# A Griffin block and an MLP in fp32 halves: eight even rounds per chunk, the second FFN ten rounds behind the first

## What is computed

```python
def _L0_attn_ref(x, norm1_w, Wx, Wy, conv_w, conv_b, Wi, Wa, lam, Wo, norm2_w, Wg, Wu, Wd):
    t = rmsnorm(x, norm1_w)
    xb = causal_depthwise_conv(t @ Wx, conv_w, conv_b)      # 4 taps
    r = sigmoid(xb @ Wa); i = sigmoid(xb @ Wi)
    a = exp(-8 * softplus(lam) * r)
    b = sqrt(maximum(1 - a * a, 1e-12)) * (i * xb)
    h = scan of h[s] = a[s] * h[s-1] + b[s] over the tokens
    h1 = x + (h * gelu(t @ Wy)) @ Wo
    u = rmsnorm(h1, norm2_w)
    return h1 + (gelu(u @ Wg) * (u @ Wu)) @ Wd              # 256 -> 1024 -> 256

x = layernorm(x + _L0_attn_ref(x, ...))
x = layernorm(x + relu(x @ W1 + b1) @ W2 + b2)              # 256 -> 1024 -> 256
```

## Time and profile before

| | |
|---|---|
| median of 3 runs | 683.96 us (678.43 to 684.47) |
| the profiled execution | 684.14 us, span 682.3 us, granted clock 0.974 |
| busy: TensorE, VectorE, GpSimd, ScalarE | 625.8, 425.5, 284.6, 252.9 us |
| first gate product of chunk 0 | 60.8 us |
| on the chain that ended last | PE 59%, DVE 22%, ACT 9%, issue 6%, POOL 2% |

### The profile page before, as it was taken

How to read it: one execution, slowest core, us unless ns; L and a number is a source line. 1 busy time by engine, 2 the same in 40 slices (tenths; PEclk the granted TensorE clock), 3 DMA queues, 4 the chain that set the end, 5 groups by cost and what they waited for, 6 DMA issues and landing times.

```text
span 682.3 us, 10001 instructions
## 1 busy us (share of the span) xinstructions
PE 625.8 (92%) x3689; PEld 553.2 (81%) x3689; DVE 425.5 (62%) x704; ACT 252.9 (37%) x484; POOL 284.6 (42%) x399
## 2 busy tenths in 40 slices
PE   7878999899989999899988999899998999898786
PEld 7777897888878898788978898788988888786766
DVE  5993568556695567656595466755595566854332
ACT  5523237223550328223461337323372336411030
POOL 2934415541364514543263423734165413643141
PEclk9989999899999999899998999899998999999989
DMA  8400000000100001000000000000000000000000
GB/s 293 162 1 2 0 32 1 1 31 2 32 1 30 3 1 32 1 31 1 32 0 18 16 1 32 0 32 1 32 0 1 32 1 0 1 33 0 1 1 31
DMA packets 13067, 15.71 MB, mean 23 GB/s; under 512 B 584, under 2 KB 12256, under 8 KB 13024
## 3 DMA queue, kind: packets, MB, share of 16 engines
q1 hardware_dynamic: 13024, 15.09, 6.5%
HBM read 10.89 MB, written 4.19 MB: 22 GB/s over the span
## 4 chain that ended last, share of the span: by engine, by line
PE 59%; DVE 22%; ACT 9%; issue 6%; POOL 2%; POOLq 0%; DVEq 0%; ACTq 0%
PE psum L303 12%; PE psum L305 11%; PE psum L304 11%; PE psum L314 8%; PE psum L316 8%; PE psum L315 8%; DVE units_lo L748 7%; DVE xv L680 2%; DVE uT_lo L695 2%; ACT decay L514 2%; DVE gy L689 2%; DVE row L720 2%; DVE uT_lo L632 1%; PE psum L324 1%; ACT L533 1%
## 5 line engine op out<-in xcount | busy, mean ns | idle before, releaser
L946 POOL TENSOR_SCALAR units_hi<-ring 128x512 fp32r<-128x512 f32 x128 | 115.4, 911 | 140.3 <-DVE ring L743 101.7
L748 DVE TENSOR_TENSOR units_lo<-ring,units_hi 128x512 fp32r<-128x512 f32 x128 | 104.6, 839 | 16.2 <-POOL units_hi L946 16.2
L314 PE MATMUL psum<-w_hi,units_hi 128*128 128x256 f32 x256 | 77.4, 302 | 20.1 <-DVE units_lo L748 20.1
L743 DVE TENSOR_TENSOR ring<-psum,ring 128x512 f32<-128x512 f32 x64 | 44.2, 691 | 79.8 <-PE psum L305 79.8
L554 ACT ACTIVATE ring<-psum 128x512 f32<-128x512 f32 x64 | 38.2, 597 | 133.0 <-PE psum L305 94.8
L316 PE MATMUL psum<-w_hi,units_lo 128*128 128x256 f32 x256 | 76.1, 297 | 0.0
L315 PE MATMUL psum<-w_lo,units_hi 128*128 128x256 f32 x256 | 76.0, 297 | 0.0
L314 PE MATMUL psum<-w_d_hi,units_hi 128*128 128x256 f32 x256 | 72.5, 283 | 2.7 <-DVE units_lo L748 2.7
L316 PE MATMUL psum<-w_d_hi,units_lo 128*128 128x256 f32 x256 | 71.6, 280 | 0.0
L315 PE MATMUL psum<-w_d_lo,units_hi 128*128 128x256 f32 x256 | 71.6, 280 | 0.0
L314 PEld LDWEIGHTS psum<-w_hi,units_hi 128*128 128x128 f32 x256 | 52.8, 206 | 22.0 <-DVE units_lo L748 22.0
(11 more groups left out here) (140 smaller groups left out, 1549.0 us busy)
## 6 DMA issues: line engine op xcount, KB each, us to landing
xs<-in_L_attn_x_dram SPq DMA_DIRECT2D x8, 512.0 KB, 3.5
out_dram<-row SPq DMA_DIRECT2D x16, 256.0 KB, 2.1
raw_weights<-in_L_ffn_W_dram SPq DMA_DIRECT2D x2, 1024.0 KB, 7.2
raw_weights<-in_L_attn_Wg_dram SPq DMA_DIRECT2D x1, 1024.0 KB, 7.9
raw_weights<-in_L_attn_Wu_dram SPq DMA_DIRECT2D x1, 1024.0 KB, 10.0
raw_weights<-in_L_attn_Wd_dram SPq DMA_DIRECT2D x1, 1024.0 KB, 12.7
raw_weights<-in_L_attn_Wx_dram SPq DMA_DIRECT2D x1, 256.0 KB, 2.7
raw_weights<-in_L_attn_Wy_dram SPq DMA_DIRECT2D x1, 256.0 KB, 3.0
```

The lines of the kernel that those rows point to most:

```text
L314: nc.tensor.matmul(dst, hi[:, k, toks], w_hi[n][:, k, :], start=(k == 0), stop=False)
L743: nc.vector.tensor_tensor(ring[:, m % RING, :], psum[2 * (m % 2) + 1][:, :], ring[:, m % RING, :], ALU.mult).then_inc(gu_ready, 1)
L748: nc.vector.tensor_tensor(units_lo[:, m, :], ring[:, m % RING, :], units_hi[:, m, :].bitcast(FP32), ALU.subtract).then_inc(ready, 1)
L946: nc.gpsimd.tensor_scalar(units_hi[:, m, :], ring[:, m % RING, :], 1.0, 0.0, ALU.mult, ALU.add).then_inc(ready, 1)
```

## The change

The loops and `period` are gone. Every engine walks through rounds r = 8p + m, written out without a loop: p is the period and m the unit. In round r TensorE makes the gate and up products of unit r, takes unit r-1 down (`down`), makes the W1 product of unit r-10 (`mlp_up`, `LAG_UP`) and takes unit r-11 down through W2 (`mlp_down`, `LAG_DOWN`). Wd and W2 accumulate unit by unit, each in two banks of its own. The mixing of chunk p+1 is laid out over the rounds of period p: transposes of t and Wx in round 0, Wa and Wi in 3, Wy in 4, Wo in 5, transposes of u in 7 (in period 0, Wo and the transposes of u both in 7). Transposes of x1 of chunk p-1 stand in round 1. Eleven rounds follow the last unit of the first FFN.

The gate now has bank 0 alone, and up and W1 share bank 1, until the last rounds, in which W1 alternates between 0 and 1. The ring of four and the eight units are replaced by two slots for each FFN: `gu_raw`, `gu_hi`, `gu_lo` and `hid_raw`, `hid_hi`, `hid_lo`. x1 has halves of its own, and `h1`, `row` and the layernorm's small tiles are doubled; h1 + x is kept in `h1`. GpSimd copies the high halves of both FFNs (`gate_hi`, `hidden_hi`), and VectorE subtracts (`gate_lo`, `hidden_lo`), unit by unit in the round. The next chunk's t is normalised in round 7 of the period before.

Ahead of the rounds, ScalarE makes the high halves of all weights but Wg; the low halves of Wd, W1 and W2 are made in rounds 0, 2 and 3; VectorE's lambda chain stands behind the convolution; W1 and W2 are loaded at once; `keep_running` has smaller counts.

```diff
-RING = 4
+SLOTS = 2
+LAG_UP = 10
+LAG_DOWN = 11
...
+                if r >= 1:
+                    pe.wait_ge(gelu_ready, r)
+                product(psum[GATE][:, :], "g", m, uT_hi, uT_lo).then_inc(gate_done, 1)
+                if r >= 1:
+                    pe.wait_ge(gu_ready, r)
+                if r > LAG_UP:
+                    pe.wait_ge(relu_ready, r - LAG_UP)
+                product(psum[UP][:, :], "u", m, uT_hi, uT_lo).then_inc(up_done, 1)
...
+            def mlp_up(w):
+                c, m = divmod(w, KH)
+                r = w + LAG_UP
+                if m == 0:
+                    pe.wait_ge(x1T_lo_ready, 2 * c + 2)
+                if r < UNITS:
+                    pe.wait_ge(gu_ready, r + 1)
...
-            def period(c, mixing):
-                for m in range(KH - 1):
-                    gate_up(c, m)
-                if mixing:
-                    transpose_t(after(c))
-                gate_up(c, KH - 1)
-                if mixing:
-                    mix_x(after(c))
-                down(c)
-                if mixing:
-                    mix_gates(after(c))
-                transpose_x1(c)
-                if mixing:
-                    mix_y(after(c))
-                mlp_up(c, mixing)
-                if mixing:
-                    mix_out(after(c))
-                mlp_down(c, range(TT - 1))
-                if mixing:
-                    transpose_u(after(c))
-                mlp_down(c, range(TT - 1, TT))
...
+            def round_of(r):
+                p, m = divmod(r, KH)
+                n = p + 1
+                mixing = n < CHUNKS
+                if units(r):
+                    gate_up(r)
+                if mixing and m == 0:
+                    transpose_t(n)
+                if mixing and m == 3:
+                    mix_decay(n)
+                if mixing and m == 7:
+                    if p == 0:
+                        mix_out(n)
+                    else:
+                        transpose_u(n)
+                if r == 1:
+                    split_done("d")
+                if units(r - 1):
+                    down(r - 1)
+                if mixing and m == 3:
+                    mix_input(n)
+                if r == LAG_UP:
+                    split_done("1", "2")
+                if units(r - LAG_UP):
+                    mlp_up(r - LAG_UP)
+                if units(r - LAG_DOWN):
+                    mlp_down(r - LAG_DOWN)
+                if mixing and m == 0:
+                    mix_x(n)
+                if p >= 1 and m == 1 and p <= CHUNKS:
+                    transpose_x1(p - 1)
+                if mixing and m == 4:
+                    mix_y(n)
+                if mixing and m == 5 and p >= 1:
+                    mix_out(n)
+                if mixing and m == 7 and p == 0:
+                    transpose_u(n)
```

More of the change, by code:

```diff
@@ L357, in mix_out @@
                 for tt in range(TT):
-                    last = product_by_tokens(half_bank(4, tt), "o", tt, uT_hi, uT_lo)
+                    for k in range(KD):
+                        last = product_by_tokens(half_bank(MIX, tt), "o", k, tT_hi[:, k, toks(tt)],
+                                                 tT_lo[:, k, toks(tt)], k == 0 and tt % 2 == 0, k == KD - 1)
                     if tt % 2:
@@ new lines, in mlp_down @@
+            def mlp_down(w):
+                c, m = divmod(w, KH)
+                pe.wait_ge(hid_lo_ready, w + 1)
+                if m == 0 and c >= 1:
+                    pe.wait_ge(s2_ready, 2 * c)
+                for tt in range(TT):
+                    last = product_by_tokens(half_bank(SECOND, tt), "2", m, hid_hi[:, w % SLOTS, toks(tt)],
+                                             hid_lo[:, w % SLOTS, toks(tt)], m == 0 and tt % 2 == 0, m == KH - 1)
+                last.then_inc(e_done, 1)
@@ L817, in _ @@
             dve.wait_ge(vecs_ready, 1)
+            weight_lo("x", "n1")
+            split_lo(tT_lo, tT_hi, tT_hi_ready, tT_lo_ready, 0)
+            weight_lo("y", "n1")
+            weight_lo("a")
+            weight_lo("i")
+            for step in range(LOOKBACK):
+                convolve(0, step)
+            xb_lo(0)
             lams = vecs[:, VECS["lam"]:VECS["lam"] + KD]
@@ L832, in _ @@
                                            ALU.add).then_inc(consts_ready, 1)
[L834 to L843 removed]
+            weight_lo("g", "n2")
             weight_lo("o")
[L845 removed]
@@ L846, in _ @@
-            weight_lo("d")
-            scan_input(first)
+            room(0)
+            weight_lo("u", "n2")
+            gated_input(0)
             for m in range(KD):
-                scan(first, m)
-            gated(first)
-            hy_lo(first)
-            weight_lo("1")
-            add_mix(first)
-            weight_lo("2")
-            split_lo(uT_lo, uT_hi, uT_hi_ready, uT_lo_ready, first)
-            with dve.Fori(0, CHUNKS // 2 - 1) as pair:
-                period((pair, 0), True)
-                period((pair, 1), True)
@@ L860, in _ @@
-            period((CHUNKS // 2 - 1, 0), True)
-            period((CHUNKS // 2 - 1, 1), False)
+                scan_input(0, m)
+            for m in range(KD):
+                scan(0, m)
+            gated(0)
+            hy_lo(0)
+            add_mix(0)
+            split_lo(uT_lo, uT_hi, uT_hi_ready, uT_lo_ready, 0)
+            for r in range(CHUNKS * KH + 2 * KH + 5):
+                round_of(r)
         @block.gpsimd
         def _(pool):
-            def carry():
-                pool.sem_inc(pool_carried, 1)
@@ new lines, in round_of @@
+            def round_of(r):
+                p, m = divmod(r, KH)
+                n, f, s = p + 1, p - 1, p - 2
+                mixing, first, second = n < CHUNKS, 0 <= f < CHUNKS, 0 <= s < CHUNKS
+                if mixing:
+                    if m == 0:
+                        head(n)
+                    if m == 1:
+                        tail(n)
+                if m == 2 and first:
+                    add_b2(f)
+                if r < UNITS:
+                    gate_hi(r)
+                if m == 0 and first:
+                    for q in range(PAIRS):
+                        ln_scale(f, 0, q)
+                if 0 <= r - LAG_UP < UNITS:
+                    hidden_hi(r - LAG_UP)
+                if m == 3 and second:
+                    for q in range(PAIRS):
+                        ln_scale(s, 1, q)
+                if mixing:
+                    if m == 5:
+                        hy_hi(n)
+                    if m == (6 if p >= 1 else 7):
+                        norm_u(n)
+                        if n + 1 < CHUNKS:
+                            rms(n + 1, ss1, x_squared, rms1_ms, rstd1, rms1_rstd)
+                    if m == 7:
+                        if n + 1 < CHUNKS:
+                            norm_t(n + 1)
+                        add_x_h1(n)
```

965 lines of the change are left out of this document (496 added, 469 removed).

## The result

The changed kernel takes 691.29 us in the median of four runs (691.23 to 692.31). Runs of the kernel before beside it gave 683.63 (678.43 to 684.47). The ratio is 1.013, 95% interval 1.008 to 1.018: it is slower by 1.3%, 7.7 us, and 4.3 above the forecast of 687.

The account below looks back on a forecast made before the run. TensorE, busy 92%, was taken to bound the kernel through its streaming and waits. Rounds beginning at 55.3 plus a loop of 630 gave a span of 685.3, with 1.8 around it 687 us; range 670 to 706.

Parts of the forecast that it names:

- A: Likeliest case: waits are exchanged, each steady wait having a named successor; 677 to 691 us, chance 0.40.
- B: Slower: VectorE's queue falls behind, each chain ending 0.65 later, some 2.5 us a period; 704 us, chance 0.25.
- C: Slower: each change between steps of 512 and 256 columns on TensorE costs 0.1 us; 701 us, chance 0.12.
- start of the rounds: Prologue gains 5.5 us together, 3.2 of it VectorE's last convolution steps without GpSimd's weight copies; rounds begin at 55.3.
- The Wo wait: Round 5: TensorE waits 2.8 us for both halves of the gated h, copied behind GpSimd's hidden copy.
- the later end: Under the skill's whole-instruction lock, round 5's gated-h chain would end at V+4.35, not V+4.1; sum 1.2 us higher.
- The waits of u: Rounds 6 and 7: u is ready at V+5.1, wanted at V+4.1, behind GpSimd's hidden copy; wait 1.1 us.
- the clock: Steady periods: the wait before Wo drops TensorE's clock to its lower level, costing 1.6 us a period.
- that of the first rounds: Rounds 0 to 2: waits of 0.5 and 0.4 on gate multiplications, plus 0.1 per restart; together 1.1 us.
- the clock in periods 0 and 1: Clock loss charged at 2.3 us in period 0 and 1.6 us in period 1.
- margin of 0.44: Bank shared by up and W1: gate multiplication can end 0.97 us after up's issue, must by 1.41.
- D: Faster: the new waits never drop the clock, so nine or ten losses of 1.6 go; 672 us, chance 0.23.

Follow-up runs that it names:

- e8: Changed kernel with an extra VectorE copy of the up product's bank ahead of every gate multiplication, ending it 0.65 us later; 710.1 us.
- e1: Changed kernel with GpSimd's two copies of the gated h moved ahead of its hidden copy in round 5; 675.8 us.
- e5: Changed kernel with nine unused identity products ahead of each Wo product's wait in periods 1 to 6, the wait not shortened; 682.0 us.
- e2: Changed kernel with GpSimd's root and four products for u moved ahead of its hidden copy in round 6, periods 1 to 6; 674.3 us.
- e10: Kernel before, loop written out, with ScalarE instead of GpSimd copying the second FFN's high halves, order otherwise untouched; 662.4 us.
- e4: Kernel before with its loop of two periods written out on each engine and no other edit; 680.3 us.
- e3: Changed kernel with the moves of e1 and e2 both made; 667.2 us.
- e6: Changed kernel with ScalarE instead of GpSimd copying the second FFN's high halves, no order changed; 658.2 us.
- e7: e3 with period 0 mostly in the other periods' order and GpSimd's first-layernorm roots behind round 0's hidden copy; 658.1 us.
- e9: e6's ScalarE copies with e7's orders, and period 1's last two convolution steps moved behind round 2's gate multiplication; 648.5 us.
- e11: e9 with 35 more identity products filling waits ahead of and inside round 0, no wait shortened; 644.3 us.

## Why the prediction was right, and where it was off

By its mechanism the likeliest case, A, is what happened: the waits were exchanged, and the steady period is what it was. By its number it was a near miss: 691.3 is 0.3 above A's own 677 to 691, and 1.3% slower is in the class that the prediction had given to B and C, not in A's "within 1%". What was missed lies in periods 0 and 1. By its steps:

| part | forecast | measured |
|---|---|---|
| start of the rounds | 55.3 | 54.1 |
| period 0 | 61.6 | 64.1 |
| period 1 | 73.6 | 77.7 |
| periods 2 to 6 | 389.5 | 390.1 |
| period 7 | 59.5 | 58.1 |
| the end | 46 | 45.2 |

**The start.** VectorE's last five convolution steps take 3.40 as expected, without GpSimd's weight copies beside them.

**Steady periods: the sum right, three terms off.** The Wo wait was put at 2.8 and is 2.38. GpSimd's two copies and the subtractions ahead of it, in the changed kernel:

```profile
251.21 1.20 POOL L957 TENSOR_SCALAR tT_hi<-gy 128x512 fp32r<-128x512 f32 x2
```
```profile
251.86 1.69 DVE L726 TENSOR_TENSOR tT_lo<-gy,tT_hi 128x512 fp32r<-128x512 f32 x2 [1.74 <-POOL tT_hi L957]
```

That is not the 1.97 and 2.11 of the earlier trace rows. The forecast let the second copy be slowed by the first subtraction. In fact the copy starts 0.07 before the subtraction and keeps its 0.62; only the subtraction is held, to 1.08. The Trainium skill's lock (SBUF — State Buffer, SBUF: two separate sides) goes to whichever starts first, and that agrees with these two; the later end that the prediction worked out from it did not come. The waits of u (1.1 forecast, 1.23) and the clock (1.6, five times in six) came as said; that of the first rounds was put at 1.1 and is 0.45. What fills the gap is small: about 0.1 for each first step behind a wait and at a few changes of width, 1.4 us in a period (76.8 measured, less 71.3 and 4.06), which I had charged only in the first rounds. That the sum came within 0.4 is in part luck: waits 0.9 too long against 1.4 that had no term. On rounds 1 and 2 the working was wrong in place: round 1's sum and roots stall nothing, round 2's multiplication 0.45.

**The term that failed: the clock in periods 0 and 1.** I charged 2.3 and 1.6. In period 0 streaming (46.9) and the four waits (1.57, 3.64, 4.07, 1.41, together 10.7, less than the 12.4 forecast) leave 6.5 for clock and restarts; its granted clock is 0.90. In period 1, 64.4 and the waits (0.16, 3.27, 2.38, 1.25) leave 6.2, where I had 1.6. There are stretches at the lower level behind the start, behind 103.38, on both sides of 118.26, behind 140.70 and behind Wo, and I had counted one a period. The two terms are 8.8 too small; the waits were 2.2 shorter than forecast, which leaves 6.6, and the start, period 7 and the end gave 3.4 back.

**B, VectorE's queue, did not come.** The copy's median fell from 0.888 to 0.623 in the first FFN and 0.617 in the second, since copies and subtractions no longer stand in one line. Its margin of 0.44 was right (e8), and in the steady periods its condition, over 0.44 late, is met in round 2 alone.

**C, the changes of width, fell.** The changed kernel at such a change:

```profile
227.15 0.39 PE L274 MATMUL psum<-mT_hi,w_a_lo 128*128 128x512 f32 x1
227.38 0.28 PE L280 MATMUL psum<-w_d_hi,gu_hi 128*128 128x256 f32 x1
227.50 0.28 PE L281 MATMUL psum<-w_d_lo,gu_hi 128*128 128x256 f32 x1
```

0.23 and 0.12, the paces of the earlier trace rows. The Trainium skill (TensorE: Matmul & The Clock Gate, step on LDWEIGHTS) lets weight loads be pulled ahead of running matmuls, and the zero here agrees with that.

**D, the clock stays up, was nearer than its 0.23 says.** The new waits did drop it, behind five Wo products of six. With 1.0 us off the wait (e1) or a fill in it (e5) the clock stayed up behind all six; with the wait untouched it stayed up behind four in e2 and in e8. So the 1.6 is no fixed price of a wait of 2.38.

**Where the expected gain of even rounds went.** The change takes the copies and subtractions of the units off TensorE's path, as said. But it puts the gated h and u behind a hidden copy in GpSimd's queue, at 1.0 and 1.2 us, and leaves a wait behind which the clock falls again. With ScalarE copying, the kernel before gets 662.4 and the changed one 658.2, less than the new prologue gives. My reading of the wait of 2.55 as a chain, not as GpSimd's line of six (e10), is why I looked at the orders and not at who copies.

## What to carry to other kernels

When a wait ends on the last of a row of equal copies, compare their pace (1.02) with the shortest of their kind (0.61) before calling it a chain; here moving them to ScalarE, 38% busy, gave 33 us where two new places in the queue gave 24, and 18 in the old order. Price each wait of TensorE with the clock that it may take along: here 1 us less idle time gave 2.5 in a period that had lost the clock. And in a new order, read off each engine's queue what now stands ahead of the operand with the shortest cover.

## What the runs showed of the hardware

- A copy on GpSimd and a subtraction on VectorE, in rows side by side, take 1.02 us a pair (1.05 and 1.09 each, overlapping), where the shortest alone take 0.61 and 0.66. The Trainium skill (SBUF — State Buffer, SBUF: two separate sides) calls the shared ports a lock held for the whole instruction. Whole instructions in turn would take 1.27 a pair or more, an estimate from the two shortest; the rows show about 0.4 us lost by each, not 0.6.
- A wait of TensorE of 2.36 to 2.38 us before Wo is followed by 3.2 us and more at the lower clock five times in six in the changed kernel, two in six in e2 and two in six in e8; one of 2.54 to 2.56 before W2 six times in seven in the kernel before and five in seven in e4. The waits of 1.55 to 1.59 in e10 and of 1.03 to 1.40 before Wo in e1, e3, e6, e7, e9 and e11 are never followed by it in the steady periods. By what the chip decides between equal waits stays open here.
- The clock at the rounds' start differs between kernels whose code is the same up to there: 0.50 in the first 4 us of the changed kernel, 1.00 in e3, some 2.8 us between them by the end of period 0.
